# A graph-network edge stage of one Trainium2 core: unrolled groups, first-layer rows packed by four, one one-hot tile in four on ScalarE, and pair adds spread over other stages

## What is computed

```
s = hs[idx_j]; v = hv[idx_j]                  # rows of the projected nodes
h   = softplus(f_ij @ W1 + b1) - log 2        # 20000 x 20 -> 20000 x 32
Wij = (h @ W2 + b2) * rcut_ij[:, None]        # -> 32 filters x 6, four are used
t_s1 = s * ys; t_s2 = sum_c(v * yv) / sqrt(3); t_v1 = s * yv; t_v2 = v * ys
edge = [t_s1 * W0, t_s2 * W1, t_v1 * W2, t_v2 * W3, ...]
agg  = segment_sum(edge, idx_i, 1250 nodes)
```

## Time and profile before

| what | value |
|---|---|
| median of 3 runs (lowest, highest) | 3580.43 us (3575.29, 3588.78) |
| the profiled execution: time, span | 3578.82 us, 3577.0 us |
| busy: PE, DVE, ACT, POOL | 2652.7, 2048.1, 1323.0, 1259.1 us |
| mean granted TensorE clock | 0.882 of full speed |
| pair adds in the edge stage (L344) | 80, mean 2222 ns |
| pair adds behind it (L595) | 80, mean 2150 ns |

### The profile page before, as it was taken

How to read it: one execution, slowest core, us unless ns; L and a number is a source line. 1 busy time by engine, 2 the same in 40 slices (tenths; PEclk the granted TensorE clock), 3 DMA queues, 4 the chain that set the end, 5 groups by cost and what they waited for, 6 DMA issues and landing times. The chain is left out here.

```text
span 3577.0 us, 43276 instructions
## 1 busy us (share of the span) xinstructions
PE 2652.7 (74%) x13387; PEld 2157.2 (60%) x13387; DVE 2048.1 (57%) x3774; ACT 1323.0 (37%) x2287; POOL 1259.1 (35%) x1067
## 2 busy tenths in 40 slices
PE   2789999501740831499988899888997889973998
PEld 2567777401630200478866788677886778852897
DVE  1788888573225125546754476545775457742762
ACT  1545444200100322336643366433653346530431
POOL 0888888567435320012221123211232012312430
PEclk9999999755975975699999999999999999996999
DMA  6211112262875875221022110221102211124100
GB/s 203 43 36 38 38 35 38 54 176 12 256 243 182 275 208 146 86 58 34 25 86 84 44 43 24 86 75 44 43 27 87 72 43 43 33 79 114 45 27 29
DMA packets 217533, 296.37 MB, mean 83 GB/s; under 512 B 100956, under 2 KB 125346, under 8 KB 212899
## 3 DMA queue, kind: packets, MB, share of 16 engines
q1 hardware_dynamic: 113600, 231.09, 21.4%
q0 software_dynamic: 91008, 49.50, 6.4%
q10 hardware_dynamic: 12768, 13.77, 1.1%
HBM read 226.26 MB, written 67.45 MB: 82 GB/s over the span
## 5 line engine op out<-in xcount | busy, mean ns | idle before, releaser
L2134 POOL TENSOR_SCALAR prob<-prob,rden,linked 125x1250 f32<-125x1250 f32 x160 | 223.9, 1399 | 967.9 <-DVE rden L2101 967.9
L2052 ACT CAST prob_high<-ps 125x375 fp32r<-125x375 f32 (+1 forms) x480 | 231.4, 504 | 266.7 <-PE ps L2014 262.6
L2093 DVE CUSTOM_DVE_ANT_0 prob<-ps,mask 125x1250 f32<-125x1250 f32 x160 | 233.1, 1457 | 132.2 <-PE ps L1990 118.2
L2106 DVE TENSOR_TENSOR prob_low<-ps,prob_high 125x375 fp32r<-125x375 f32 (+1 forms) x480 | 269.8, 585 | 46.7 <-ACT prob_high L2052 46.7
L2003 PE MATMUL ps<-ident,prob 125*125 125x125 f32 x1600 | 252.3, 273 | 17.3 <-POOL prob L2134 10.6
L554 PE MATMUL ps<-onehot,mhi 125*128 125x512 f32 (+1 forms) x960 | 258.6, 379 | 1.9 <-DVE onehot L500 1.9
L333 POOL DMA_INDIRECT Hg<-h_rows,idx x160 | 231.5, 1447 | 74.0 <-POOL idx L328 36.4
L2003 PEld LDWEIGHTS ps<-ident,prob 125*125 125x125 f32 x1600 | 232.4, 187 | 29.7 <-POOL prob L2134 22.9
L554 PE MATMUL ps<-onehot,mlo 125*128 125x512 f32 (+1 forms) x960 | 247.8, 368 | 0.0
L2044 ACT ACTIVATE prob<-prob,top 125x1250 f32<-125x1250 f32 x160 | 214.6, 1341 | 48.5 <-DVE top L2093 39.9
L1631 POOL TENSOR_TENSOR g_row<-g_row,bvo 125x512 f32<-125x512 f32 x80 | 104.1, 1301 | 354.1 <-DMA g_row<-g_d 352.1
(11 more groups left out here) (355 smaller groups left out, 6380.7 us busy)
## 6 DMA issues: line engine op xcount, KB each, us to landing
mask<-mask_d SPq DMA_DIRECT2D x40, 546.9 KB
wd<-L_ffn_Wd SPq DMA_DIRECT2D x84, 256.0 KB, 4.2
wu<-L_ffn_Wu SPq DMA_DIRECT2D x84, 256.0 KB, 4.0
g_row<-g_d SPq DMA_DIRECT2D x80, 250.0 KB
g_d<-g_row SPq DMA_DIRECT2D x70, 250.0 KB
sg_wd<-L_ffn_Wd SPq DMA_DIRECT2D x16, 1024.0 KB, 6.7
pairs<-zeros SPq DMA_DIRECT2D x18, 625.0 KB
y_slots<-u_y ACTq DMA_DIRECT2D x84, 128.0 KB, 3.7
```

What stands on the lines that cost most here:

```text
L2052: s.copy(M.pt[0][:, n % 3, 0:w], T.ps[0:P, 3 + n % 4, 0:w]).then_inc(high, 1)
L2093: v.tensor_tensor_reduce(M.prob[:, r, :], S(u)[0:P, 0:N], M.mask[:, it % MASKS, :], 1.0, 3.0e38, ALU.add, ALU.min, M.top[:, r:r + 1]).then ...
L2106: v.tensor_tensor(M.pt[1][:, n % 3, 0:w], T.ps[0:P, 3 + n % 4, 0:w], M.pt[0][:, n % 3, 0:w].bitcast(F32), ALU.subtract).then_inc(low, 1)
L2134: nc.gpsimd.tensor_scalar(M.prob[:, r, :], M.prob[:, r, :], M.rden[:, r:r + 1], T.linked[:, it:it + 1], ALU.mult, ALU.mult).then_inc(norme ...
```

## The change

Every engine's program of the edge stage is written out for all 40 groups, without loops. The edge weight is multiplied once into `a4` in the first stage; `wr` and its instruction are gone, and the messages read the filter product from bank 5. The hidden products of four groups accumulate in one bank on 128 partitions (weights padded with zeros), so `bend`, `softplus` and `act_sum` run once in four groups; features are turned eight groups ahead. The second bias is a product of its own ahead of the filter product. The features are turned straight from `a20`, and the row fetch takes its index from `dsti`; GpSimd's copies are gone. One one-hot tile in four (j = 3) is made on ScalarE as relu(1 - |n - src|). `mlo` moves up behind `prior`. The sums of the last chunk of both halves share bank 4. Of the pair adds 60 are issued in the edge stage, 14 in node_update, 20 in expert_norm, 16 in route, 6 in experts_down, 20 in splines (two behind each tile) and 24 in experts_up (one behind every third block).

```diff
+SG, LOOK = 4, 8
+EARLY_ADDS = 60
...
-                    sp.dma_start(E.w1[:], A["L0_gnn_W1"]).then_inc(w2_in, 16)
...
-                    sp.dma_start(w2raw[FF:FF + 1, :], A["L0_gnn_b2"].rearrange("(a f) -> a f", a=1)).then_inc(w2_in, 16)
+                    sp.wait_ge(cleared, 2)
+                    for q in range(SG):
+                        r = slice(q * FF, (q + 1) * FF)
+                        sp.dma_start(E.w1[:, q, r], A["L0_gnn_W1"]).then_inc(w2_in, 16)
+                        sp.dma_start(E.b1[r, :], A["L0_gnn_b1"].rearrange("(f a) -> f a", a=1)).then_inc(w2_in, 16)
+                        sp.dma_start(w2raw[r, :], A["L0_gnn_W2"]).then_inc(w2_in, 16)
+                    for r in (0, 32):
+                        sp.dma_start(b2raw[r:r + 1, :], A["L0_gnn_b2"].rearrange("(a f) -> a f", a=1)).then_inc(w2_in, 16)
...
+                    nc.vector.tensor_tensor(E.a4[:], E.a4[:], E.rw[:].unsqueeze(2).broadcast_to([P, ET, 4]), ALU.mult)
...
+                    def fetch(g):
+                        if g >= 2:
+                            pool.wait_ge(hg_free, g - 1)
                         for j in range(EG):
...
+                            c = EG * g + j
+                            nc.gpsimd.indirect_dma_start(
+                                Hg[:, g % 2, j, :, :].rearrange("p c f -> p (c f)"), None, h_rows[:, :],
+                                bass.IndirectOffsetOnAxis(dsti[:, c:c + 1], 0)).then_inc(hg_in[g % 2], 16)
+                    fetch(0)
+                    fetch(1)
                     pool.wait_ge(T.zeroed, 2 * ZEROING)
...
+                    n = 0
+                    for g in range(NG):
+                        if g + 2 < NG:
+                            fetch(g + 2)
+                        more = EARLY_ADDS * (g + 1) // NG
+                        pool.wait_ge(idx_ready, more // EG + 1)
+                        pair_adds(pool, nc, T, pairs, n, more)
+                        n = more
...
+                    def features(g):
+                        act.wait_ge(f_turned, g + 1)
+                        if g >= 2:
+                            act.wait_ge(h_made, g - 1)
+                        s.copy(f20T[:, g % 2, :], T.ps[0:FR, 6, 0:EG * P]).then_inc(fT_ready, 1)
+                    def bend(q):
+                        act.wait_ge(h_made, SG * q + SG)
+                        if q >= 1:
+                            act.wait_ge(h_ready, q)
+                        s.activation(sa[:], T.ps[:, 7, 0:EG * P], ACT.Abs, bias=E.b1[:]).then_inc(bent, 1)
+                        s.activation(pre[:], T.ps[:, 7, 0:EG * P], ACT.Relu, bias=E.b1[:]).then_inc(bent, 1)
...
+                    def high(g):
                         act.wait_ge(msg_ready, g + 1)
...
+                        if g >= 2:
+                            act.wait_ge(hot_used, EG * (g - 1))
+                        s.copy(mhi[:, g % 2, :, :], msg[:, g % 2, :, :, :].rearrange("p j c f -> p j (c f)")).then_inc(hi_ready, 1)
+                    def hot(g):
+                        c = EG * g + EG - 1
+                        if g >= 1:
+                            act.wait_ge(hot_used, EG * g)
+                            act.wait_ge(last_hot, g)
+                        s.activation(away[:], T.iota_n[0:P, :], ACT.Abs, bias=minus[:, c:c + 1]).then_inc(far, 1)
+                        act.wait_ge(far, g + 2)
+                        s.activation(onehot[:, EG - 1, :], away[:], ACT.Relu, bias=T.ones[0:P, 0:1], scale=-1.0).then_inc(last_hot, 1)
...
+                    for g in range(SG):
+                        features(g)
                     bend(0)
                     softplus(0)
...
+                    for g in range(SG, LOOK - 1):
+                        features(g)
+                    act.wait_ge(far, 1)
+                    for g in range(NG):
+                        if g + LOOK - 1 < NG:
+                            features(g + LOOK - 1)
+                        q, r = divmod(g + LOOK - 2, SG)
+                        ends = r == SG - 1 and g + LOOK - 2 < NG
+                        if ends:
+                            bend(q)
+                        high(g)
+                        if ends:
+                            softplus(q)
+                        hot(g)
...
+                    def hot(g, j):
+                        if g >= 1:
+                            dve.wait_ge(hot_used, EG * (g - 1) + j + 1)
+                        v.tensor_scalar(onehot[:, j, :], T.iota_n[0:P, :], srcf[:, EG * g + j:EG * g + j + 1],
+                                        None, ALU.is_equal).then_inc(hot_ready, 1)
+                    def act_sum(q):
+                        dve.wait_ge(soft_step, 2 * q + 2)
+                        v.scalar_tensor_tensor(hT[:, q % 2, :], sa[:], -LOG2, pre[:], ALU.add, ALU.add).then_inc(h_ready, 1)
+                    def messages(g):
...
+                        if g >= 1:
                             hot(g - 1, 1)
...
+                        dve.wait_ge(hg_in[u], (g // 2 + 1) * EG * 16)
+                        step(v.tensor_tensor(q3[:], V, yv, ALU.mult))
                         dve.wait_ge(w_made, g + 1)
...
+                        step(v.tensor_tensor(u02[:], W[:, :, 0:3:2, :], S.broadcast_to([P, EG, 2, FF]), ALU.mult))
+                        step(v.tensor_tensor(v3[:], W[:, :, 3:4, :].broadcast_to([P, EG, 3, FF]), V, ALU.mult))
                         settle()
                         v.sem_inc(hg_free, 1)
...
+                        if g >= 1:
                             hot(g - 1, 2)
...
                         step(v.tensor_tensor(qs[:], q3[:, :, 0, :], q3[:, :, 1, :], ALU.add))
...
+                        step(v.tensor_tensor(M[:, :, 0, :], u02[:, :, 0, :], y0, ALU.mult))
                         step(v.tensor_tensor(M[:, :, 2:8:2, :], u02[:, :, 1:2, :].broadcast_to([P, EG, 3, FF]), yv, ALU.mult))
                         settle()
                         step(v.tensor_tensor(qs[:], qs[:], q3[:, :, 2, :], ALU.add))
...
                         step(v.tensor_tensor(M[:, :, 3:8:2, :], v3[:], ys, ALU.mult))
                         settle()
...
+                        step(v.scalar_tensor_tensor(M[:, :, 1, :], qs[:], 1.0 / math.sqrt(3.0), W[:, :, 1, :], ALU.mult, ALU.mult))
                         settle()
+                        v.sem_inc(w_free, 1)
                         v.sem_inc(msg_ready, 1)
...
+                        dve.wait_ge(keyrow_in[u], (g // 2 + 1) * 16)
+                        step(v.tensor_tensor(same[:], keyrow[:, u, :, :], kcol.unsqueeze(2).broadcast_to([P, EG, P]), ALU.is_equal))
                         settle()
...
+                        v.sem_inc(keyrow_free, 1)
                         step(v.tensor_tensor(prior[:], same[:], T.lower[:].unsqueeze(1).broadcast_to([P, EG, P]), ALU.mult))
...
                         dve.wait_ge(hi_ready, g + 1)
+                        if g >= 2:
+                            dve.wait_ge(hot_used, EG * (g - 1))
                         v.tensor_tensor(mlo[:, u, :, :], M.rearrange("p j c f -> p j (c f)"),
                                         mhi[:, u, :, :].bitcast(F32), ALU.subtract).then_inc(lo_ready, 1)
                         settle()
...
+                        step(v.tensor_reduce(early[:], prior[:], AX.X, ALU.add))
+                        step(v.tensor_scalar(kd[:], kcol, T.iota_p[:, 0:1], None, ALU.subtract))
+                        step(v.tensor_reduce(E.late_cnt[:, tiles(g)], same[:], AX.X, ALU.add))
+                        settle()
+                        step(v.scalar_tensor_tensor(kf[:], early[:], 0.0, kd[:], ALU.is_equal, ALU.mult))
+                        settle()
+                        step(v.tensor_scalar(E.late_idx[:, tiles(g)], kf[:], T.iota_p[:, 0:1], None, ALU.add))
+                        settle()
+                        v.sem_inc(idx_ready, 1)
+                    act_sum(0)
+                    for g in range(NG):
+                        messages(g)
+                        hot(g, 0)
+                        q, r = divmod(g + 2, SG)
+                        if r == 0 and SG * q < NG:
+                            act_sum(q)
+                    for j in (1, 2):
+                        hot(NG - 1, j)
...
+                    def turn(g):
+                        if g >= 1:
+                            pe.wait_ge(fT_ready, g)
                         for j in range(EG):
...
+                            ins = nc.tensor.transpose(T.ps[0:FR, 6, j * P:(j + 1) * P], a20[:, EG * g + j, :], T.ident[0:P, 0:P])
                         ins.then_inc(f_turned, 1)
...
+                    def hidden(g):
+                        q, r = divmod(g, SG)
                         pe.wait_ge(fT_ready, g + 1)
...
+                        if r == 0 and q >= 1:
+                            pe.wait_ge(bent, 2 * q)
+                        nc.tensor.matmul(T.ps[:, 7, 0:EG * P], E.w1[:, r, :], f20T[:, g % 2, :], start=r == 0,
+                                         stop=r == SG - 1).then_inc(h_made, 1)
```

(48 more changed lines are left out.)

325 lines of the change are left out of this document (83 added, 242 removed).

## The result

The changed kernel takes 3520.11 us (median of 4 runs, 3515.59 to 3525.81), the kernel before 3579.23 us (4 runs, 3575.29 to 3588.78). The ratio is 0.9826, 95% interval 0.9811 to 0.9841: 1.7% faster. The forecast was 3519 us. The profiled execution took 3519.71 us, its span is 3518.0.

A forecast was written before the change was run, and what follows sets the result against it. VectorE was taken to set the edge stage's period, with TensorE and GpSimd nearly full. Edge stage -44, expert_norm -20.5, experts_down +4.5, splines -10, experts_up +10 make -60: 3578.8 - 60 = 3519 us, range 3500 to 3540.

The forecast's parts named there:

- Edge stage, from the first to the last scatter product: Edge stage: 40 groups at TensorE's 12.35 us, with small corrections 492 us; the stage ends at 617, -44 us.
- The last eight groups: End of the edge stage: groups without transposes run at VectorE's 11.8 us, -4 us.
- VectorE: 11.8 us a group: Edge stage: VectorE's period falls from 13.86 to 11.8 us a group, bounds 11.4 and 13.0.
- The rival with VectorE as the bound through mhi: Edge stage: VectorE waits for mhi, 13.0 us a group, -16 instead of -44, total 3547 us; chance 0.17.
- GpSimd under TensorE: Edge stage: GpSimd needs 10.4 us a group with 1.5 adds, under TensorE's 12.35.
- Start of the stage: Edge stage: more transposes and hidden products before the first filter product; first scatter product some 12 us late, near 125.
- expert_norm: expert_norm: pair adds fall from 34 to 20, the store of xf then closes the stage, -20.5 us.
- route 0 and experts_down +4.5: route keeps 16 adds, 0 us; experts_down gets 6 instead of 4 before the first row fetch, +4.5 us.
- splines: splines: 12 adds in front become 2 a tile, GpSimd 7.3 us a tile against VectorE's 6.1; -10 us (-18 to +3).
- experts_up: experts_up: 24 adds, one per three blocks, beside the row loads, +10 us (0 to 25).
- The rival with 2.27 each: experts_up: the 24 adds come out in full, 54 us instead of 10, total 3563 us; chance 0.10.
- the slower one with 6 each: experts_up: row loads wait for each add to land, 24 x 6 = 143 us, total 3652 us; chance 0.05.

The follow-up runs named there:

- e2: Changed kernel without the product that adds the second bias to the filter values; 3508.7 us, ratio 0.9799 to the kernel before.
- e3: Changed kernel with the fourth one-hot tile made on VectorE again instead of ScalarE; 3533.7 us, ratio 0.9868 to the kernel before.
- e11: Changed kernel with the edge weight multiplied into the filter values once a group again; 3528.8 us, ratio 0.9852 to the kernel before.
- e12: Changed kernel with the edits of e3 and e11 together; 3542.0 us, ratio 0.9884 to the kernel before.
- e5: Changed kernel with 80 pair adds in the edge stage instead of 60 and none in splines instead of 20; 3505.1 us, ratio 0.9776 to before.
- e1: Changed kernel with the first filter product issued ahead of the transposes and hidden products of groups 4 to 6; 3520.0 us, ratio 0.9836 to before.
- e6: Changed kernel with e1's edit, and first mhi and group 0's one-hot tiles made earlier on ScalarE and VectorE; 3520.1 us, ratio 0.9825 to before.
- e8: Changed kernel with e5 and e6 joined and later adds 14, 25, 15, 0, 0, 26 (node_update to experts_up); 3496.3 us, ratio 0.9763 to before.
- e4: Changed kernel with 34 pair adds in expert_norm instead of 20 and 10 in experts_up instead of 24; 3545.9 us, ratio 0.9900 to before.

## Why the prediction was right

- **Edge stage, from the first to the last scatter product: 492 forecast, 491.8 measured.** The mechanism is shown: VectorE gave up its place as the bound and TensorE took it, at 100% busy and clock 1.00; e2 moves the stage with TensorE's work, e3 and e11 leave its middle groups as they are, e12 marks where VectorE takes over. That the number fits to 0.2 us is luck. The bias product was mis-sized (0.25 forecast, 0.42 measured), so a middle group has 12.57 instead of 12.35, which is +9 in 40 groups. The last eight groups were to run at VectorE's 11.8 and save 4; they took 87 us, 13 less than eight middle ones, because TensorE without transposes and hidden products needs 10.95 and VectorE kept up. The first microseconds at the slow clock cost 2.5, where 2 was forecast.
- **VectorE: 11.8 us a group forecast, 11.2 measured**, so before u it waits 1.15 us on average, where 0.3 to 0.7 was forecast. The 0.2 for mlo's wait was half of that: 2.0 us in the second group and then 0.5 in every fourth, 5.5 in all 40 groups. The rival with VectorE as the bound through mhi is refuted.
- **GpSimd under TensorE: right for 60 adds, with less room than worked out.** 1.5 adds a group took 89.8 of 120 us, and with 0.30 at each of 53 issues 11.1 us a group, where 10.4 was forecast. My sum for two would have been 11.5; e5's window has 102.63 busy, and with 0.30 at each of 58 issues that is the whole 120.
- **Start of the stage: +12 forecast, +16.6 measured.** This is the term with the largest error inside the stage. The first transpose came at 89.65 instead of 87.95, where the input stage was costed at nothing; from it to the filter product it was 28.4 us, where the slow clock gave 27.3 in my sum and I had gone part of the way to the fast clock's 22, but all of it ran slow; the last 11.5 are as forecast. e1 and e6 show that 9 of the 16.6 are an order of issue.
- **expert_norm: -20.5 forecast, -24.9 to the start of route.** The store closes it, as said, and 25 adds bring the adds back as the last (e8). The missing 4 us are the landing of the last add: before, the stage closed 4.2 us behind the last add's end (817.8, route at 822.05), and the forecast set the end of the store against the end of the add.
- **route 0 and experts_down +4.5:** to the first row fetch it is +7.0 (74.8 to 81.8). Of this route has 1.9, where its adds now end behind the slots, for which GpSimd used to wait 0.4 us, and the two more adds 5.2.
- **splines: -10 forecast, -0.4 measured.** Two things were wrong. The terms of the forecast add up to less than its 10: -19.8, six tiles at 1.2 to 1.5, and two adds of 2.27 behind the last are -6 to -8. And "7.3 against 6.1" is too small: an add took 2.31 + 0.3 there, a table fetch 1.1 + 0.3, a scatter 1.24 + 0.3, 8.2 a tile in sum. What the 12 adds in front had cost was right (120.9 before, 101.6 in e5, which has none); the 20 that replaced them cost as much.
- **experts_up: +10 forecast, +7.2 measured**, 0.30 us an add. Eight profiles with these 24 adds have 141.6 to 146.6 us against 136.2 and 135.3 without, so an add costs 0.2 to 0.5. The rival with 2.27 each and the slower one with 6 each are refuted by the same stretch and by e4. On the Trainium skill, "DMA: Bandwidth & Descriptors", Specifications, as the forecast cited it: small transfers may be inefficient by themselves, but 24 adds of 4-byte elements beside loads at 260 GB/s cost 7 us.
- The total fits better than its terms, and that too is luck: against the forecast, +4.6 at the start, +0.7 in route and experts_down and +9.6 in splines were made up by -4.4 in expert_norm, -2.8 in experts_up and -6.7 in stages that the change leaves alone.

## What to carry to other kernels

Work out each engine's own need for a period, not only the longest: here TensorE's was 12.57 and VectorE's 11.2, so undoing one part of the change left the middle groups as they were, and undoing both did not. And do it again for the groups at the end, where an engine has less to do. A background transfer has no price of its own; it costs what it holds up behind it on its queue, which went from nothing to over 2 us between stages, so put it where its queue is idle and count its real spacing there. A longer look-ahead has a prologue: issue the first useful product as soon as its input is there, and put the rest of the look-ahead behind it.
